# Other steps for taps, means, variance, experts and masks in the last stage, and GpSimd's product with C written one column to the left

## What is computed

```python
h = unfold3(t, 2) @ proj_w.T + proj_b                 # (4, 3136, 768)
x = layernorm(h)
Bp, Cp = x @ W_B + b_B, x @ W_C + b_C                 # 16 states
delta = softplus(x @ W_D + b_D + p_Delta)             # per token and channel
A_bar = exp(delta * A);  B_bar = (A_bar - A) / (delta * A) * delta * Bp
s = A_bar * s + B_bar * x                             # scan over tokens
y = sum over the 16 states of Cp * s
h = h + y
z = layernorm(h)
route = softmax(z @ enc_w @ sw_w + ...)               # largest of 8 wins
h = h + (gelu(z @ w1[e] + b1[e]) @ w2[e] + b2[e]) * largest probability
```

## Time and profile before

| | |
|---|---|
| median of 3 runs | 9070.57 us |
| profiled execution | 9071.86 us |
| its span, first to last instruction | 9070.1 us |
| mean granted TensorE clock | 0.916 |
| busy over the span: PE, DVE, ACT, POOL | 85%, 68%, 47%, 66% |
| POOL in the last stage | 9 tenths or more of most slices |
| x with B, and v with C (POOL) | 672 each, 3680 and 3681 ns |
| decays (ACT) | 2688, 627 ns |
| weighings (DVE) | 2688, 671 ns |
| scans (DVE) | 1344, 2028 ns |

### The profile page before, as it was taken

One profiled execution on the slowest core, in us unless ns is written; L12 is line 12 of the kernel. 1 busy time (PEld: TensorE's weight loads), 2 busy tenths in 40 slices (PEclk: granted clock), 3 DMA queues, 4 the chain that ended last, 5 costly groups with the idle time before them and its releaser, 6 DMA issues.

```text
span 9070.1 us, 86859 instructions
## 1 busy us (share of the span) xinstructions
PE 7693.1 (85%) x31228; PEld 3214.3 (35%) x31228; DVE 6124.9 (68%) x6499; ACT 4306.6 (47%) x7641; POOL 5969.4 (66%) x2484
## 2 busy tenths in 40 slices
PE   6799999776999996588788888788887888888887
PEld 3444444322444432133333333333333333333333
DVE  1355555442233333988888888888888888888885
ACT  1366666553344432445544445444445444454442
POOL 0011111115766640998999989999989999899995
PEclk9999999998999997799889998899988899988988
DMA  0011111114544432223233223333232332233331
GB/s 26 22 41 45 39 44 41 31 31 83 104 100 100 99 65 68 95 98 119 96 120 115 100 96 119 106 112 116 94 119 96 123 112 100 99 116 106 117 110 50
DMA packets 356855, 786.60 MB, mean 87 GB/s; under 512 B 70437, under 2 KB 282806, under 8 KB 348936
## 3 DMA queue, kind: packets, MB, share of 16 engines
q1 hardware_dynamic: 320376, 690.75, 25.0%
q0 software_dynamic: 21712, 51.75, 2.2%
q10 hardware_dynamic: 14336, 38.54, 1.2%
HBM read 597.36 MB, written 183.35 MB: 86 GB/s over the span
## 4 chain that ended last, share of the span: by engine, by line
PE 34%; DVE 14%; ACT 5%; issue 5%; POOL 2%; DMA 0%; SPq 0%; DVEq 0%; ACTq 0%; POOLq 0%
PE ps L1527 7%; DVE v L1880 6%; PE ps L1635 6%; DVE v L1871 6%; PE ps L1534 5%; PE ps L1532 5%; PE ps L1573 3%; ACT ps L1762 3%; PE ps L1523 2%; PE ps L1638 2%; PE ps L1636 2%; PE ps L1577 1%; POOL v L1482 1%; POOL v L1494 1%; DVE dl L1861 1%
## 5 line engine op out<-in xcount | busy, mean ns | idle before, releaser
L1880 DVE TENSOR_TENSOR_SCAN v<-ps,v 128x898 f32<-128x898 f32 x1344 | 2725.5, 2028 | 92.4
L1494 POOL TENSOR_TENSOR v<-v,ct 128x1792 f32<-128x1792 f32 x672 | 2473.8, 3681 | 447.6 <-ACT st L1723 447.6
L1482 POOL TENSOR_TENSOR v<-xr,bt 128x1792 f32<-128x1792 f32 x672 | 2472.8, 3680 | 97.3 <-DMA xr<-h_by_channel 97.3
L1762 ACT ACTIVATE ps<-dr,aa 128x448 f32<-128x448 f32 x2688 | 1585.6, 627 | 1526.7 <-DVE v L1880 1509.5
L1871 DVE SCALAR_TENSOR_TENSOR v<-ps,aa,v 128x448 f32<-128x448 f32 x2688 | 1690.5, 671 | 553.6 <-ACT ps L1762 527.1
L222 POOL DMA_DIRECT2D tokens<-ob x448 | 235.4, 532 | 1878.2 <-ACT ob L383 1827.4
L1635 PE MATMUL ps<-w_or_w,gm 128*112 128x384 f32 x1792 | 719.9, 551 | 370.1 <-DVE gm L1957 277.5
L1573 PE MATMUL ps<-v,dg 128*32 128x448 f32 x5376 | 705.8, 599 | 206.9 <-POOL v L1494 106.3
L1635 PEld LDWEIGHTS ps<-w_or_w,gm 128*112 128x112 f32 x1792 | 334.0, 197 | 768.7 <-DVE gm L1957 319.9
L1527 PE MATMUL ps<-h,w_or_w 128*128 128x448 f32 x1344 | 536.8, 549 | 16.3 <-DVE gm L1924 16.3
L1532 PE MATMUL ps<-x,wpa 128*128 128x448 f32 x1008 | 445.3, 577 | 17.2 <-ACT h L1688 10.2
(11 more groups left out here) (324 smaller groups left out, 11919.9 us busy)
## 6 DMA issues: line engine op xcount, KB each, us to landing
xr<-h_by_channel SPq DMA_DIRECT2D x168, 896.0 KB, 7.3
dr<-delta_by_channel SPq DMA_DIRECT2D x168, 896.0 KB, 6.3
x<-tokens SPq DMA_DIRECT2D x252, 224.0 KB, 5.3
tokens<-ob POOLq DMA_DIRECT2D x448, 112.0 KB, 2.4
w_or_w<-in_w SPq DMA_DIRECT2D x29, 1536.0 KB, 6.4
w_or_w<-centred_w SPq DMA_DIRECT2D x27, 1536.0 KB, 6.4
h_by_channel<-h SPq DMA_DIRECT2D x112, 336.0 KB, 10.9
delta_by_channel<-dl SPq DMA_DIRECT2D x112, 336.0 KB, 4.8
```

Source lines behind the costliest of these rows:

```text
L1482: tt(v[:, n % RING, :, 1:T + 1], xr[:, dc % 2, 1:].rearrange("p (i t) -> p i t", i=4), bt[:, q:q + 1, :].to_broadcast([128, 4, T]), ALU.mu ...
L1494: tt(v[:, n % RING, :, 1:T + 1], v[:, n % RING, :, 1:T + 1], ct[:, q:q + 1, :].to_broadcast([128, 4, T]), ALU.mult).then_inc(s_cm, 1)
L1762: fn(decay(g), dr[:, dc % 2, g, :], ACT.Exp, scale=aa[:, 4 * k + g:4 * k + g + 1]).then_inc(s_a, 1)
L1880: nc.vector.tensor_tensor_scan(row, flat[:, 1024 * pair:1024 * pair + 2 * T + 2], row, 0.0, ALU.mult, ALU.add).then_inc(s_sc, 1)
```

## The change

Four things in `tail`, and nothing elsewhere:

1. The table of slots. Taps move three slots ahead, P_PJ from 1 to -2, A_HW from 5 to 2: the taps of chunks 0 and 1 of a unit stand in slots 22 and 23 of the unit two before it (`front(i + 2, k - STEPS)`). Means, variance, C and B, experts, masks, outputs and copies move by a slot or two, as the diff shows.
2. `weigh_out` writes columns 0 to T - 1 instead of 1 to T, and PE's `step` reads these. Column T stays, so it waits for the scan (`s_sc`) and no longer for `s_st`.
3. `weigh_in` waits also for `s_st` of the slot six before, since it overwrites column T.
4. PE's loop calls `front` for negative slots.

```diff
@@ -1327,15 +1327,15 @@
         s_oa = sem("t_out_written")
         s_out = [sem("t_out_stored_even"), sem("t_out_stored_odd")]
 
-        P_PJ, P_MU, P_VAR, P_Z, P_BC = 1, 7, (8, 10), 11, 9
-        A_HW, A_MU, A_SQ, A_RS, A_MX, A_SP = 5, 11, (9, 13), 14, (16, 17), (17, 18)
+        P_PJ, P_MU, P_VAR, P_Z, P_BC = -2, 5, (7, 9), 11, 10
+        A_HW, A_MU, A_SQ, A_RS, A_MX, A_SP = 2, 9, (7, 11), 13, (16, 17), (17, 18)
         V_Z, V_BC, V_DL = 15, 14, (18, 19)
-        P_SQ, P_MEAN, P_ENC, P_IN, P_LOG, P_TURN = (0, 2), 1, 4, 5, 6, 10
-        P_MASK, P_OUT = (12, 13, 14, 15), (16, 17, 18, 18, 19, 20, 21, 22)
+        P_SQ, P_MEAN, P_ENC, P_IN, P_LOG, P_TURN = (0, 2), 1, 4, 6, 6, 10
+        P_MASK, P_OUT = (11, 12, 13, 14), (16, 17, 18, 18, 19, 20, 20, 21)
         A_SQ2, A_MS, A_RS2, A_EX, A_GL = (2, 4), 5, 7, 11, 14
-        A_OUT = (21, 22, 23, 23, 24, 25, 26, 27)
-        V_VAR, V_ENC, V_IN, V_LOG, V_EQ, V_OH, V_MASK = 6, 8, 9, 10, 12, 14, (16, 17, 18, 19)
-        ROUTE, TAIL = 9, 28
+        A_OUT = (21, 22, 23, 23, 24, 25, 25, 26)
+        V_VAR, V_ENC, V_IN, V_LOG, V_EQ, V_OH, V_MASK = 6, 8, 10, 10, 12, 13, (15, 16, 17, 18)
+        ROUTE, TAIL = 9, 27
 
         def means(i):
 
@@ -1479,6 +1479,7 @@
                     pool.wait_ge(s_xr[dc % 2], 16 * ((DC // 2) * i + dc // 2 + 1))
                 n = STEPS * i + k
                 after(pool, s_ns, n + 1 - RING)
+                after(pool, s_st, n + 1 - RING)
                 tt(v[:, n % RING, :, 1:T + 1], xr[:, dc % 2, 1:].rearrange("p (i t) -> p i t", i=4), bt[:, q:q + 1, :].to_broadcast([128, 4, T]),
                    ALU.mult).then_inc(s_v, 1)
 
@@ -1490,8 +1491,8 @@
                 if k in OWN:
                     return
                 n = STEPS * i + k
-                pool.wait_ge(s_st, others(n))
-                tt(v[:, n % RING, :, 1:T + 1], v[:, n % RING, :, 1:T + 1], ct[:, q:q + 1, :].to_broadcast([128, 4, T]),
+                pool.wait_ge(s_sc, 2 * others(n))
+                tt(v[:, n % RING, :, 0:T], v[:, n % RING, :, 1:T + 1], ct[:, q:q + 1, :].to_broadcast([128, 4, T]),
                    ALU.mult).then_inc(s_cm, 1)
 
             pool.memset(x3[:, :, :], 0.0).then_inc(s_set, 1)
@@ -1570,7 +1571,7 @@
                 else:
                     pe.wait_ge(s_cm, others(n))
                 for g in range(4):
-                    last = mm(ps[32 * g:32 * g + 32, YB, 0:T], dg[:, 4 * k + g, :], v[:, n % RING, g, 1:T + 1],
+                    last = mm(ps[32 * g:32 * g + 32, YB, 0:T], dg[:, 4 * k + g, :], v[:, n % RING, g, 0:T],
                               start=(q == 0), stop=False)
                 last.then_inc(s_ns, 1)
                 if q == Q - 1:
@@ -1652,8 +1653,10 @@
             last.then_inc(s_pm, 1)
             pe.wait_ge(s_dgm, 1)
             pe.wait_ge(s_pd, 16)
-            for k in range(STEPS):
+            for k in range(P_PJ, STEPS):
                 front(0, k)
+            for k in range(P_PJ, 0):
+                front(1, k)
             for i in range(UNITS + 1):
                 for k in range(TAIL if i == UNITS else STEPS):
                     if i < UNITS:
@@ -1664,6 +1667,8 @@
                         mlp(i - 1, k)
                     if i + 1 < UNITS:
                         front(i + 1, k)
+                    if i + 2 < UNITS and k >= STEPS + P_PJ:
+                        front(i + 2, k - STEPS)
 
         @block.scalar
         def _(act):
```

## The result

| | before | changed |
|---|---|---|
| median, same chip | 9075.05 us (9055.2 to 9088.93, 15 runs) | 9096.59 us (9075.41 to 9112.64, 15 runs) |
| ratio | | 1.0021, 95% interval 1.0013 to 1.0029 |
| profiled execution, span | 9071.86, 9070.1 | 9099.0, 9097.2 |
| mean granted clock of TensorE | 0.916 | 0.910 |

The changed kernel is slower by 0.2%, 21.5 us: just over the bound of 0.2% set for a measurable difference, with an interval of 0.13 to 0.29%. The forecast was 9097 for the profiled execution, 1.3 less for the median: it came out at 9099.0 and 9096.59. What follows is about whether it was right for the reasons it gave.

The account below looks back on a forecast made before the run. Bound: TensorE's late taps, delaying ScalarE's decays, VectorE's scans, then GpSimd. Path 191.15 + 1.1 + 0.5 = 192.75 us against 191.8: +0.95 x 26 units = +25, so 9071.86 becomes 9097 us; 8-in-10 range 8995 to 9165.

Parts of the forecast that it names:

- The rows down to 191.15: VectorE's first weigh per slot, followed from slot 22 to the next slot 22, forecast at 191.15 us.
- a mean loss of 1.1 at output 4: TensorE's products of output 4 run slower after a 3.4 us wait, now on the path: +1.1 us a unit.
- 0.5 at the fourth experts' inputs: Clock loss on TensorE after a 2.6 us wait before the fourth experts' product: between 0 and 2.3, taken as 0.5.
- First and last unit: First unit (TensorE starts 4 us later, has slack) and last unit of the last stage: counted as nothing.
- Gain 0.4 us: Masks one slot earlier, copies of outputs 0 to 3 staying: VectorE's slot 23 at 10.1 instead of 10.5.
- A gain of 9.5: From slot 7 to the next slot 22: 125.8 us before, 116.35 with the change.
- ScalarE's waits for taps fall by half: Sign to look for: ScalarE's waits for taps, 503.0 us in 18 units before, fall by half.
- the waits for the sums of states: Sign to look for: ScalarE's waits for the sums of states, 209.7 us in 18 units, do not fall.
- The loss after the 4.8 us: TensorE's clock loss after idling before the second experts' product (4.6 us forecast): 2.0 (of 2.3) put in the path.
- the upper end: All clock losses at their highest (2.6, 2.8, 2.3): 196.4 us a unit, +119 us, 9191 us.
- rival 1: TensorE keeps its clock and the change gains: period 189 to 190.5, 9000 to 9040 us; chance 0.27.
- rival 3: A new wait in slots 7 to 14 decides, much slower: 196.4 us a unit, 9150 to 9191 us; chance 0.17.

Follow-up runs that it names:

- run 1: The kernel before with only GpSimd's shifted write (product with C one column left, waiting for the scan): 9081.22 us, ratio 1.000 to the kernel before.
- run 2: The changed kernel with the old product with C, so only the table of slots is changed: 9096.30 us, ratio 1.0018 to the kernel before.
- run 6: The changed kernel with copies one slot earlier, second squares at slot 12 and the old product with C: 8737.92 us, ratio 0.9627 to the kernel before.
- run 5: The changed kernel with all copies of outputs one slot earlier and the second squares at slot 12: 8737.72 us, ratio 0.9621 to the kernel before.
- run 10: The kernel before with taps, means and masks at the changed slots; variance, experts and GpSimd's write stay old: 9068.38 us, ratio 0.9993.
- run 4: The changed kernel with ScalarE's second squares in slot 12 instead of 11: 9048.01 us, ratio 0.9965 to the kernel before.
- run 12: The changed kernel with taps and the taps for the means back at their old slots: 8969.30 us, ratio 0.9883 to the kernel before.

## Why the prediction was right, point by point

| slot, zero at 22 | forecast | short unit | long unit |
|---|---|---|---|
| 23 | 10.1 | 10.1 | 10.4 |
| 3 | 40.6 | 40.8 | 43.8 |
| 7 | 74.8 | 74.9 | 78.0 |
| 12 | 113.7 | 113.0 | 116.6 |
| 13 | 121.9 | 121.0 | 124.6 |
| 22 | 191.15 | 190.3 | 195.4 |
| mean period, with the clock's losses | 192.75 | 192.85 | |

*The path held.* The rows down to 191.15 hold no loss of the clock at output 4, and the short unit has none there. It follows them to within 0.9 us at every slot. The long unit is 3.0 behind the short one at slot 3, since output 4 lost the clock there (below), and 5.1 at the end; from slot 3 to 7 both take 34.1 where 34.2 were forecast. The idle time of TensorE before the experts' inputs was to be 4.6 and is 4.8. ScalarE's waits in this stretch, at its squares of slot 11 and its deviation:

```profile
6797.31 0.58 ACT L1685 ACTIVATE sq<-h 128x448 f32<-128x448 f32 x1 [6.83 <-PE ps L1524]
...
6816.43 0.63 ACT L1705 ACTIVATE rs<-ps,eps 128x448 f32<-128x448 f32 x1 [7.76 <-PE ps L1524]
```

*The clock: sum right by luck, pattern not.* I took a mean loss of 1.1 at output 4, and 0.5 at the fourth experts' inputs. TensorE's timeline of the changed kernel, output 4 in units that follow each other, then the experts' inputs behind a wait in a short and in a long unit:

```profile
6310.27 5.46 PE L1636 MATMUL ps<-w_or_w,gm 128*112 128x384 f32 x8 [3.43 <-ACT ot L1801]
...
6505.41 2.83 PE L1636 MATMUL ps<-w_or_w,gm 128*112 128x384 f32 x8 [3.43 <-ACT ot L1801]
```

```profile
6596.28 6.24 PE L1528 MATMUL ps<-h,w_or_w 128*128 128x448 f32 x12 [4.82 <-DVE gm L1929]
...
6613.94 4.78 PE L1528 MATMUL ps<-h,w_or_w 128*128 128x448 f32 x12 [2.67 <-DVE gm L1929]
...
6789.61 6.85 PE L1528 MATMUL ps<-h,w_or_w 128*128 128x448 f32 x12 [4.82 <-DVE gm L1929]
...
6807.88 6.26 PE L1528 MATMUL ps<-h,w_or_w 128*128 128x448 f32 x12 [2.67 <-DVE gm L1929]
```

Two stretches at output 4, length, busy PE, PEld, DVE, ACT, POOL, then the granted clock: 0.50 of full in a long unit, 1.00 in a short one.

```profile
6310.30:6315.70 5.40, 5.40 (x9) 2.32 (x9) 5.37 (x5) 2.03 (x5) 4.07 (x2) 0.50 0.85 268
...
6505.50:6508.20 2.70, 2.70 (x9) 1.27 (x9) 2.70 (x3) 1.30 (x4) 2.70 (x2) 1.00 0.78 204
```

After the same wait of 3.43 the products take 5.46 and 2.83 in turn, a mean loss of 1.3. After the same 2.67 they take 4.78 in the short unit, with none lost, and 6.26 in the long one: 1.5 in every other unit, 0.75 for the 0.5. In both, a wait of 4.82 and slow products (6.24 and 6.85) lie just before. The short unit, 190.3, is 0.9 under the forecast path of 191.15, and the mean period is 2.6 above the short unit where 1.6 was added for the clock: two errors of one microsecond that cancel. A figure for a single unit would not have come out.

*First and last unit: not nothing.* The products for the means of the last three units, before and in the changed kernel:

```profile
8624.08 4.78 PE L1527 MATMUL ps<-h,jm 128*128 128x448 f32 x12
...
8987.80 4.67 PE L1527 MATMUL ps<-h,jm 128*128 128x448 f32 x12
```

```profile
8668.73 4.78 PE L1528 MATMUL ps<-h,jm 128*128 128x448 f32 x12
...
9016.67 4.67 PE L1528 MATMUL ps<-h,jm 128*128 128x448 f32 x12
```

These last two periods take 363.7 us before and 347.9 now, 15.8 less, a term that the prediction put at nothing. The 25 periods ahead of them took 27.7 us more (4794.4 to 4822.1), where the forecast had 0.95 us for each of 26, 25 in all. So the last stage grew by 11.4 us in this pair (by 20.8 from run 1 to run 2, with the one unit of 197.8 in it) and not by 25, and the profiled execution still came out at 9099 because the stages before it happened to take 15.8 us longer in it. Direction and period were forecast for the reasons given; that the total is within 2 us is luck.

*GpSimd.* As forecast, its wait is for the scan, 14.1 us a unit (253.7 over 18; 15 forecast), the product takes 3.68, and nothing follows from it: runs 1, 2 and 6. The changed kernel's stretch of one unit, columns as in the earlier trace rows:

```profile
6679.00:6871.85 192.85, 166.54 (x560) 66.53 (x560) 165.28 (x172) 92.73 (x196) 173.52 (x48) 0.87 0.31 106
```

GpSimd has the most busy time, 173.52 of 192.85 us. The Trainium skill (Perfetto Trace Analysis, "Identifying the Most-Contended Engine") would take the engine with the highest occupancy first; here an earlier release of it was worth nothing, at 92% busy (run 1, 174.74 of 190 us) and at 97% (run 5 against run 6). No run made GpSimd's own work shorter.

*What was wrong in it.* "Gain 0.4 us" for the masks was right for slot 23 and wrong as the part's worth: alone it is 3.7 us a unit (191.65 to 187.92). I followed the outputs only as far as slot 23, and did not ask what output 7's earlier place and copy give on TensorE in slots 23 and 0; in the sum this did not show, because from slot 23 on I followed the taps' queue, which takes that slack. "A gain of 9.5" after slot 7 was given to taps, experts and variance together; from slot 7 to the next slot 23 it is 135.9 us before, 123.8 in run 10, and 125.7 and 127.5 in the changed kernel's short and long unit, so with the new taps the steps of experts and variance take from that gain (1.6 of the mean period, 191.23 to 192.85). "ScalarE's waits for taps fall by half" was a third (45% with the taps for the means), and the waits for the sums of states, which were not to fall, went from 209.7 to 179.7. The loss after the 4.8 us is 2.0 in the path and 2.3 in the range, and the upper end adds up to 196.55, not 196.4; neither moves the forecast. The period of rival 1 (189 to 190.5) is that of every second unit, though TensorE does not keep its clock there either (6.24), and that of rival 3 (196.4) is nearly that of the others. So the time was right, and the split of it over the parts was not: the sum was made along one path, and says nothing of what a part would give alone.

*A version that beats both.* Early copies and the second squares at slot 12, with the rest of the change: 8737.72, 3.8% under the kernel before.

## What to carry over

When a change moves several things in a fixed order shared by engines, follow the path once for the whole and once with each part taken out: here a part worth 81 us alone and one worth 40 alone gave 5 together, and 315 once the copies stood earlier too. What is queued behind an instruction that waits for a buffer (here the copies that free an output's bank) is where earlier work stops paying: move what frees the buffer first. Read what a change of a repeated part is worth from its period, and look at the first and last repetition apart. An engine's occupancy does not tell whether it is waited for; a row of waits for it does.

## What was not expected of the hardware

In these runs the granted clock's losses follow a pattern of the whole period and are no independent draws: after the same 3.43 us of wait output 4's products took 2.83, 4.53 or 5.46 in the kernel before, 5.46 and 2.83 in strict turn in the changed one (units of 190.6 and 195.1 us), and 5.46 in every unit looked at in run 4. Nor do the wait and slow products just before tell it. The fourth experts' inputs in run 12:

```profile
6722.30 6.30 PE L1528 MATMUL ps<-h,w_or_w 128*128 128x448 f32 x12 [2.68 <-DVE gm L1925]
```

They take 6.2 to 6.3 after 2.68 us of wait in 17 of 19 units of run 12 (the records of the other two are incomplete), with products at full speed (4.78) ahead of the wait, and 4.78 in the short units of the changed kernel, with slow ones (6.24) ahead. A step that removes one wait can fix such a pattern at its dear or its cheap end: run 4's output 4 lost 1.3 us a unit of the mean more than the changed kernel's. What makes a given unit lose it was not tried apart from the table's moves, and stays open.
